# Node update in rounds of one chunk, gates gathered early, weighted rows of the first pass in PSUM

## What is computed

```python
msgs = z[edge_dst] @ Wd + z[edge_src] @ Ws + edge_weight[:, None] * ww[None, :] + bm
agg  = jax.ops.segment_max(msgs, edge_dst, num_segments=n)
hidden = relu(z @ W1a + where(deg > 0, agg, 0) @ W1b + b1)
x = layernorm(x + hidden @ W2 + b2)                  # node update, layer 0
h = x @ node_fc_W + node_fc_b                        # layer 1
a = sum(h[src] * h[dst]); alpha = seg_softmax(a, dst)
g = sigmoid(einsum(relu(he @ W1_m + b1_m), W2_m) + b2_m); beta = seg_softmax(g, dst)
h_att = segment_sum(alpha * (h[src] @ node_att_W[k]), dst) / 3
h_rel = segment_sum(sum_m beta_m * (h[src] @ rel_att_W[m]), dst) / 3
```

## Time and profile before

| | us |
|---|---|
| median of 3 runs | 2271.08 |
| lowest, highest | 2266.31, 2273.05 |
| profiled execution, its own time | 2279.13 |
| its span | 2277.4 |
| GpSimd busy | 1643.7 (72%) |
| TensorE busy | 1658.0 (73%) |
| VectorE busy | 1326.4 (58%) |
| ACT busy | 1119.3 (49%) |

### The profile page before, as it was taken

One profiled execution on the slowest core, in us unless ns is written; L12 is line 12 of the kernel. 1 busy time (PEld: TensorE's weight loads), 2 busy tenths in 40 slices (PEclk: granted clock), 3 DMA queues, 4 the chain that ended last, 5 costly groups with the idle time before them and its releaser, 6 DMA issues. The chain is left out here.

```text
span 2277.4 us, 43250 instructions
## 1 busy us (share of the span) xinstructions
PE 1658.0 (73%) x9891; PEld 1016.1 (45%) x9891; DVE 1326.4 (58%) x5220; ACT 1119.3 (49%) x3305; POOL 1643.7 (72%) x1705
## 2 busy tenths in 40 slices
PE   4687777778777887860767777776777776778774
PEld 4222222222232222210636666665666665667574
DVE  4665555555554444444656656666666666666559
ACT  1243433334434444540556656655565666556548
POOL 3777777777777777775657777777777777777625
PEclk7799999999988999985979988899888889888978
DMA  8634434343433343432432222222222222222214
GB/s 255 205 126 143 130 127 129 125 145 127 144 108 125 128 139 111 144 128 82 128 108 67 65 63 63 66 65 65 66 63 64 65 66 66 60 65 66 65 47 124
DMA packets 115983, 235.04 MB, mean 103 GB/s; under 512 B 32909, under 2 KB 68230, under 8 KB 106422
## 3 DMA queue, kind: packets, MB, share of 16 engines
q0 software_dynamic: 52832, 109.39, 19.9%
q1 hardware_dynamic: 56522, 97.21, 11.6%
q10 hardware_dynamic: 6540, 27.42, 3.4%
HBM read 166.01 MB, written 67.89 MB: 103 GB/s over the span
## 5 line engine op out<-in xcount | busy, mean ns | idle before, releaser
L209 POOL DMA_INDIRECT acc<-d_src_product,b_region x784 | 772.0, 985 | 239.4 <-issue 217.4
L463 POOL DMA_INDIRECT d_region<-d_h,d_region x784 | 758.1, 967 | 248.4 <-issue 216.1
L859 DVE SCALAR_TENSOR_TENSOR acc<-b_region,acc 128x128 f32<-128x128 f32 x784 | 271.7, 347 | 456.4 <-DMA acc<-d_src_product,b_region 456.1
L1577 DVE TENSOR_TENSOR acc<-acc,banks 128x160 f32 x784 | 252.6, 322 | 231.0 <-PE banks L1379 93.0
L651 PE MATMUL banks<-acc,b_region 64*128 64x512 f32 x1176 | 321.9, 655 | 38.3 <-ACT gate_col L756 17.9
L1345 PE MATMUL banks<-shift_ident,d_region 128*128 128x128 f32 x784 | 136.0, 299 | 240.7 <-DMA d_region<-d_h,d_region 231.6
L870 DVE SCALAR_TENSOR_TENSOR acc<-acc,b_region 128x128 f32<-128x128 f32 x784 | 270.2, 345 | 0.2 <-DVE acc L859 0.2
L1376 PE MATMUL banks<-d_region 128*128 128x128 f32 x1568 | 258.4, 319 | 0.0
L1379 PE MATMUL banks<-d_region,pick 128*128 128x128 f32 x1568 | 245.6, 307 | 0.0
L1376 PEld LDWEIGHTS banks<-d_region 128*128 128x128 f32 x1568 | 244.5, 236 | 0.7
L756 ACT ACTIVATE acc<-banks,b_region 128x1024 f32<-128x1024 f32 x147 | 158.8, 1112 | 167.9 <-PE banks L651 167.7
(11 more groups left out here) (261 smaller groups left out, 2394.4 us busy)
## 6 DMA issues: line engine op xcount, KB each, us to landing
d_runs<-acc SPq DMA_DIRECT2D x48, 1024.0 KB, 4.4
acc<-ea ACTq DMA_DIRECT2D x25, 1024.0 KB, 5.5
acc<-d_src_product,b_region POOLq DMA_INDIRECT x784
d_region<-d_h,d_region POOLq DMA_INDIRECT x784
d_region<-d_rel SPq DMA_DIRECT2D x49, 256.0 KB
hT<-xT SPq DMA_DIRECT2D x7, 448.0 KB, 6.9
d_src_product<-acc SPq DMA_DIRECT2D x7, 448.0 KB, 4.5
d_gates<-acc ACTq DMA_DIRECT2D x196, 6.0 KB
```

The costliest lines, as they stand in the source:

```text
L209: pool.indirect_dma_start(self.rows[:, s, j, :], None, d["B"], bass.IndirectOffsetOnAxis(self.idx[:, k:k + 1], 0)).then_inc(self.gathered[ ...
L463: pool.indirect_dma_start(rows[:, s, :], None, table, bass.IndirectOffsetOnAxis(idx[:, s:s + 1], 0)).then_inc(gathered[q], 16)
L859: nc.vector.scalar_tensor_tensor(rows[:, s, j, :], wwb, wgt[:, k:k + 1], rows[:, s, j, :], ALU.mult, ALU.add).then_inc(ch, 1)
L1577: nc.vector.tensor_tensor(w, w, UZ[q % 2][:, :, j, :], ALU.add).then_inc(ad, 1)
```

## The change

In the runs stage `step` writes its result into PSUM bank 0 (three buffers of 128 columns) and takes `ww` from the fourth quarter of that bank; `run` reads the row there. GpSimd waits for s_done of a step, no longer for r_done of a run, before it gathers into a group again. What TensorE kept in bank 0 beside the steps moves to banks 1 and 2.

In the node update every engine takes chunk n whole, then what follows the norm for chunk n - 1. GpSimd gathers the gates right after the run ends, without waits, into the same place as before; TensorE turns them at the head of the edge stage, and VectorE's second memset waits for that. In `gather_rows` the load of the iteration count comes after the first eight groups.

```diff
@@ gather_rows
-    rest = iterations_but_one(pool, t)
...
         if q == 0:
             after_first()
+    rest = iterations_but_one(pool, t)
     with pool.Fori(0, rest) as it:
@@ phase_runs
+        stepped = t["psum"][0][:, 0:STEPS * P].rearrange("p (s f) -> p s f", f=P)
+        wwp = t["psum"][0][:, STEPS * P:(STEPS + 1) * P]
...
+        def s_done(k):
+            return 2 * k if k else 1
...
-                    pool.wait_ge(ch, r_done(4 * (g - RG) + 3))
+                    pool.wait_ge(ch, s_done(GJ * (g - RG) + GJ - 1))
...
-                    last = nc.tensor.matmul(bank[0][:, k * P:(k + 1) * P], negH1[:, c * G4 + k * P:c * G4 + (k + 1) * P],
+                    last = nc.tensor.matmul(bank[1][:, k * P:(k + 1) * P], negH1[:, c * G4 + k * P:c * G4 + (k + 1) * P],
                                             w2n, start=True, stop=True)
...
                     pe.wait_ge(h2d, c)
-                    pe.wait_ge(gd, c)
+                    pe.wait_ge(h1c, c)
                 for k in range(z):
-                    nc.tensor.matmul(bank[0][:, k * P:(k + 1) * P],
+                    nc.tensor.matmul(bank[2][:, k * P:(k + 1) * P],
...
+            c.link(nc.vector.tensor_copy(wwp, wwb))
...
-                nc.vector.scalar_tensor_tensor(rows[:, s, j, :], wwb, wgt[:, k:k + 1], rows[:, s, j, :],
+                nc.vector.scalar_tensor_tensor(stepped[:, k % STEPS, :], wwp, wgt[:, k:k + 1], rows[:, s, j, :],
                                                ALU.mult, ALU.add).then_inc(ch, 1)
...
-                nc.vector.scalar_tensor_tensor(H[:, k % n, :], H[:, (k - 1) % n, :], rst[:, k:k + 1], rows[:, s, j, :],
-                                               ALU.add, ALU.max).then_inc(ch, 1)
+                nc.vector.scalar_tensor_tensor(H[:, k % n, :], H[:, (k - 1) % n, :], rst[:, k:k + 1],
+                                               stepped[:, k % STEPS, :], ALU.add, ALU.max).then_inc(ch, 1)
@@ phase_nodes0, sync
-            for c in range(NC4 + 3):
-                if c >= 3:
-                    store_h(c - 3)
-                if c < NC4:
-                    store_x1(c)
+            for c in range(NC4):
+                store_x1(c)
+                store_h(c)
@@ gpsimd
             for k in range(JC):
-                if k % 2 == 0:
-                    pool.wait_ge(hp, NC4 - JC // 2 + 1 + k // 2)
                 pool.indirect_dma_start(jg[:, k, :, :].rearrange("p m e -> p (m e)"), None, d["gates"][0:TC * P, :],
@@ tensor
-            for n in range(-3, NC4 + 2):
...
-            pe.wait_ge(jgs, 16 * JC)
...
-            turn_gates(*GATE_BANKS)
+            for n in range(NC4 + 1):
+                if n < NC4:
+                    turn_rows(n)
+                    hidden(n)
+                    out(n)
+                if n:
+                    turn_x1(n - 1)
+                    h_rows(n - 1)
@@ scalar
+            for n in range(NC4 + 1):
+                if n < NC4:
+                    copy_rows(n)
+                if n:
+                    norm(n - 1)
+                    copy_x1(n - 1)
+                if n < NC4:
+                    square_root(n)
@@ vector
+            for n in range(NC4 + 1):
+                if n < NC4:
+                    bound_hidden(n)
+                    stats_of(n)
+                if n:
+                    copy_h_rows(n - 1)
+                if n < NC4:
+                    shift(n)
@@ phase_edges, tensor
+            jg = gates_by_job(t)
+            pe.wait_ge(jgs, 16 * JC)
+            for s, b in enumerate(GATE_BANKS):
+                for k in range(4):
+                    last = nc.tensor.transpose(bank[b][:, k * P:(k + 1) * P], jg[:, s % 2 * 4 + k, s // 2, :], ident[:, :])
+                last.then_inc(gt, 1)
@@ scalar
             for s, b in enumerate(GATE_BANKS):
+                act.wait_ge(gt, s + 1)
@@ vector
             nc.vector.memset(acc[:, 0:2, :], 0.0).then_inc(zero, 1)
+            dve.wait_ge(gt, 2 * M)
             nc.vector.memset(acc[:, 2:5, :].rearrange("p a b -> p (a b)")[:, 0:(JC * M + NBLK) * P], 0.0
                              ).then_inc(zero, 1)
```

More of the change, by code:

```diff
@@ L497 @@
 HB = 3
+STEPS = 3
 LEASH = 4
@@ L686, in shifted_counts @@
                 pe.wait_ge(cnt, NBLK)
-                view = bank[0][:, 0:2 * NBLK].rearrange("p (a b) -> p a b", a=2)
+                view = bank[1][:, 0:2 * NBLK].rearrange("p (a b) -> p a b", a=2)
                 nc.tensor.matmul(view, t["shift"], cp, start=True, stop=True)
-                nc.tensor.matmul(bank[0][0:1, 2 * NBLK:4 * NBLK], ident[:, P - 1:P], cp, start=True, stop=True
+                nc.tensor.matmul(bank[1][0:1, 2 * NBLK:4 * NBLK], ident[:, P - 1:P], cp, start=True, stop=True
                                  ).then_inc(has, 1)
@@ L789, in _ @@
                         act.wait_ge(gd, c)
-                    nc.scalar.activation(hrep[:, 0:n], bank[0][:, 0:n], ACT.Copy).then_inc(hrc, 1)
+                    nc.scalar.activation(hrep[:, 0:n], bank[2][:, 0:n], ACT.Copy).then_inc(hrc, 1)
                 if 0 <= c < NC4 and off == 2:
@@ L893, in has_edges @@
                 c.link(nc.vector.scalar_tensor_tensor(total, cp[:, 0, :], float(EP), cp[:, 1, :], ALU.mult, ALU.add))
-                turned = bank[0][:, 0:4 * NBLK].rearrange("p (n a b) -> p n a b", n=2, a=2)
+                turned = bank[1][:, 0:4 * NBLK].rearrange("p (n a b) -> p n a b", n=2, a=2)
                 c.link(nc.vector.tensor_copy(cp, turned[:, 0, :, :]))
@@ L950, in blocks_view, with phase_nodes0 @@
     return bank[:, 0:(z - a) * P].rearrange("p (b f) -> p b f", f=P)
-def phase_nodes0(nc, new_sems, t, i, d):
+def phase_nodes0(nc, new_sems, t, i, d, jgs):
     with ExitStack() as ctx:
@@ L969, in phase_nodes0 @@
         fcbr = ca(P)
-        jg = cb(JC * M * P).rearrange("p (c m e) -> p c m e", c=JC, m=M)
+        cb(JC * M * P)
+        jg = gates_by_job(t)
         ends = cb(NBLK * P).rearrange("p (b f) -> p b f", f=P)
@@ L1074, in h_rows @@
                 last.then_inc(hp, 1)
[L1076 to L1080, removed]
-            for n in range(-3, NC4 + 2):
[L1083 to L1088, removed]
-                if 0 <= n - 1 < NC4:
-                    turn_x1(n - 1)
-                if 0 <= n - 2 < NC4:
-                    h_rows(n - 2)
-            pe.wait_ge(jgs, 16 * JC)
-            pe.wait_ge(mx, NC4)
-            pe.wait_ge(va, NC4)
-            pe.wait_ge(xtc, NC4)
-            turn_gates(*GATE_BANKS)
+            for n in range(NC4 + 1):
[4 more added lines that the diff above has]
+                if n:
+                    turn_x1(n - 1)
+                    h_rows(n - 1)
         @block.scalar
@@ L1130, in copy_x1 @@
                 nc.scalar.activation(x1T[:, c * G4:c * G4 + n], bank[4][:, 0:n], ACT.Copy).then_inc(xtc, 1)
-            for n in range(-3, NC4 + 2):
-                if n + 3 < NC4:
-                    copy_rows(n + 3)
-                if 0 <= n - 1 < NC4:
+            for n in range(NC4 + 1):
[3 more added lines that the diff above has]
+                    norm(n - 1)
                     copy_x1(n - 1)
-                if 0 <= n + 1 < NC4:
-                    square_root(n + 1)
-                    norm(n + 1)
+                if n < NC4:
+                    square_root(n)
         @block.vector
@@ L1197, in _ @@
             assert all(widths(c)[0] in (1, 2, 4) for c in range(NC4))
-            for n in range(-3, NC4 + 2):
-                if 0 <= n + 2 < NC4:
-                    bound_hidden(n + 2)
-                if 0 <= n + 1 < NC4:
-                    stats_of(n + 1)
-                if 0 <= n - 2 < NC4:
-                    copy_h_rows(n - 2)
-                if 0 <= n + 1 < NC4:
-                    shift(n + 1)
+            for n in range(NC4 + 1):
[6 more added lines that the diff above has]
+                    shift(n)
 def one_hot(nc, t, table, col, out):
@@ L1853, in build @@
             new_sems.phase_over()
-        phase_nodes0(nc, new_sems, t, i, d)
+        jgs, = new_sems.kept("gates_gathered")
+        phase_nodes0(nc, new_sems, t, i, d, jgs)
         new_sems.phase_over()
-        phase_edges(nc, new_sems, t, i, d)
+        phase_edges(nc, new_sems, t, i, d, jgs)
         new_sems.phase_over()
```

13 lines of the change are left out of this document (7 added, 6 removed).

## The result

The changed kernel takes **2251.53 us** (median of 22 executions, 2247.82 to 2291.8), the kernel before 2273.22 in the same company (22, 2262.77 to 2280.52): ratio 0.9905, interval 0.9896 to 0.9914, so 21.7 us faster. The profiled execution took 2248.64 for a span of 2246.9. Ratios leave out executions more than 1.5% above a kernel's fastest; of the change's 22 those are five, at 2285 to 2292, to which experiment 7 comes back.

What follows compares the result with a forecast made beforehand. GpSimd's queue of gathers was taken to bound the runs stage. Minus 29 (weighted rows), plus 10.5 (node update) and minus 0.5 (register load) made minus 19: 2260.1 us profiled, 2252 for the median, range 2238 to 2272.

Steps and rivals of the forecast that it cites:

- rival A: Whole kernel: the main forecast, unblocked gathers outweighing a slower node update, 2252 us, own range 2244 to 2262; 45%.
- Weighted rows in PSUM: Runs stage: with one SBUF tensor per step and run, gathers are no longer blocked; minus 29 us, ends 0 and minus 30.6.
- The price of PSUM operands: VectorE's steps and runs: reading or writing PSUM costs 0; other end 0.07 us more per operation.
- rival C: Runs stage: PSUM steps are longer and make gathers tied to the MLP late; plus 9, 2261 us; 15%.
- Earlier release, copy of the weights, bank moves: Runs stage: buffers freed after step, weights copied to PSUM, products in banks 1 and 2; worth nothing, hidden, and 0.
- Node update: One-chunk rounds bound by the chain of engines at 6.5 us, not gathers; plus 10.5 us, ends 0 and plus 44.
- the clock term: Node update: 2.1 rounds at TensorE's half clock, each 3.6 us longer; 7.5 us within the plus 10.5.
- Early gates: Seam between node update and edge stage: gates gathered beside the chain remove some 10 us, counted inside the node update's sum.
- Rival B: Node update: the chain keeps the gathers' pace; node update plus 2, 2244 us; 13%.
- D: Runs stage: gathers are still blocked, so only the seam counts; plus 10, 2281 us; 8%.
- F: Gathers: part of the excess stays through new alignments; 2258 to 2266 us; 10%.
- E: Node update: TensorE gets no full clock, all thirteen rounds at half clock; plus 44, 2286 us; 9%.

Runs made afterwards that it cites:

- experiment 7: The changed kernel with the edge stage's one-hots and iota also in PSUM: 2235.0 to 2281.3 us, ratio 0.9887 (first three) to the kernel before.
- experiment 1: The kernel before with only the change's runs stage (steps in PSUM, bank moves, earlier release): 2246.59 us, ratio 0.9881.
- run 337: Not a follow-up run: VectorE's `run` operation (running maximum) takes 337 ns in the changed kernel, against 345 in the kernel before.
- experiment 9: The changed kernel run once more, nothing edited: 2249.08 us, ratio 0.9888 to the kernel before.
- experiment 2: The changed kernel with the runs stage of the kernel before: 2276.3 to 2319.8 us, ratio 1.0040 (first four) to the kernel before.
- experiment 5: The changed kernel with step reading its weight from SBUF, still writing PSUM: 2260.78 us, ratio 0.9947 to the kernel before.
- experiment 6: The changed kernel with step in place in SBUF, weight from PSUM, run reading two SBUF tensors: 2258.6 to 2299.6 us, ratio 0.9954 (first three) to the kernel before.
- experiment 3: The kernel before with only the early gates and later load of the count, staggered node update kept: 2262.83 us, ratio 0.9959.
- experiment 4: The changed kernel with the node update's staggered loops and store order of the kernel before: 2236.35 us, ratio 0.9836 to the kernel before.
- experiment 10: The changed kernel with 32 and 30 idle TensorE products ahead of the node update: median 2283.76 us of twelve, ratio 0.9977 to the kernel before.
- experiment 8: The changed kernel with both the staggered node update and the edge stage's one-hots in PSUM: 2219.96 us, ratio 0.9770 to the kernel before.

## Why the prediction was right, and where its sizes were off

Forecast 2252, measured 2251.5, by the mechanism of rival A. That the numbers meet so closely is partly luck. The gain was forecast as 19 us and measured as 21.7; the kernel before stood at 2273.22 in the longer company and not at 2271.08, and the two differences nearly cancel. In the traces the sum was off by more: 2260.1 was forecast for the profiled execution, 2248.64 was measured. The two terms were off by 2 and by 5 us there, and another 5 came from the edge stage, which scatters.

**Weighted rows in PSUM: right.** Minus 29 was forecast, the trace has minus 30.7 for the stage, experiment 1 alone minus 27.3 in the medians. L209 fell to 945 where 946 to 950 was forecast, and of the ten gathers over 1.15 us one is left. The nearest row, L1577, was the right guide, though weaker than it was taken for: in the trace each of its four additions takes 322 ns and the next starts 0.45 us after it, so the gather beside them had gaps. The run of the change settles it: it reads one SBUF tensor and writes SBUF every 0.52 us with a step between, and doesn't block. The pointer scalar doesn't either; it stayed in SBUF. By the Trainium skill, "SBUF — State Buffer", section "Who interferes with whom", a VectorE instruction with two SBUF inputs contends with a GpSimd instruction that reads SBUF, and one with at most one, outside the modes that use both of VectorE's ports, doesn't. The fall from 985 to 945 agrees; no run shows which access of GpSimd is held up.

**The price of PSUM operands: right, 0.** Step 354 against 347, run 337 against 345: together 1 ns less. The other end, 0.07 us per operation (rival C), is excluded, and the leash never came into it: 6.3 us of waits against 5.3. That end was misread too: it set the time per addition of L1577 against the length of a step, and between one addition and the next lie 0.13 us in which the trace has register work, so it says nothing of an operand's price. By the Trainium skill, "VectorE: DVE Perf Modes", the TRN2 errata section, an operation from PSUM to SBUF has 120 cycles plus the elements where one from SBUF to SBUF has 58 plus the elements: 62 cycles more each time, as an estimate. The row of L875, 8 ns shorter than L870, disagrees with it for 128 columns of f32.

**Earlier release, copy of the weights, bank moves: 0, as forecast**, together. The runs part is the same 980.3 in experiment 1 and fits the blocked excess (784 x 40 ns = 31.4). They weren't tried one by one.

**Node update: the mechanism right, its cost too high for the traced execution.** Plus 10.5 less 0.5 was forecast, plus 4.9 measured (plus 6.6 in experiment 9, plus 9.9 in experiment 2). The round is 6.48, forecast 6.5; at half clock it is 3.6 longer, as forecast. What was too large is the clock term: "1.5 half-clock rounds at the start and 0.6 later: 2.1 x 3.6 = 7.5". Chunk 12 was turned 74.4 us after chunk 1 (1048.80 to 1123.19); eleven full-clock rounds are 71.3, so the clock cost 3.1 there. Past 1056.9 the stage stayed at full clock until the last chunk had been turned. This size is a lot too: the same eleven rounds cost 3.0 to 4.3 us over full clock in experiments 5, 6 and 9, 7.7 in experiment 2, which is the forecast, and 33 in experiment 7. The seam was 1.2 us shorter than the sum: the last row of h ends at 1132.0 and the first gather starts at 1135.46, 3.4 us instead of 4.6.

**Early gates: right.** "Some 10 us at the seam": experiment 3 has 10.1 in the node part and 11 in the medians, the register load among it; the 0.5 forecast for that load wasn't tried alone. The gates' gathers came 8 to 9 us later than forecast, as GpSimd now waits for the chain, and still 19 us before their use. The prediction had them only inside the sum and so did not say what the rounds cost alone. Experiment 4 does: 15 us. Its own row of 5.0 us per staggered round against 6.5 gives 12 x 1.5 = 18.

**Rival B** (chain keeps the pace) and **D** (still blocked) fell: 1.78 us waits of GpSimd in every chunk, and 945. **F** fell in the runs stage. **E**, at 9%, was put as all or nothing for the kernel. It fits single executions, as far as their totals tell: 5 of 22, at 2285 to 2292 against its 2286, and by the trace one in experiment 7 and one in experiment 10. What the argument missed is that "20 us at full clock right in this stage with gaps of 1 to 2 us" in one trace says nothing about the next execution.

**What would show it:** the rounds of 6.5 us, the end of the gathers near 1022 (1021.0) and the pitch of 0.26 came. Three gathers are over 1.1 us, the longest 1.21, where none was forecast, and L859 and L870 at 345 ns became 354 and 337. The edge stage's first gather starts 25.8 us earlier (1135.46 against 1161.26), forecast 19; the difference is the node term's 5 and the runs term's 2.

## What to carry to other kernels

Where a queue of indirect gathers sets the pace, look at VectorE's operations with two SBUF tensors before anything else on VectorE: moving one operand of each to PSUM cost VectorE nothing that shows here and gave 31 us of the traced runs stage (27 in the medians, experiment 1) and 16 in the other (experiments 4 and 8, 2236.35 to 2219.96). A stage that waits in turn on several engines is safer staggered: in experiment 1 three rounds wholly at half clock (1041.54 to 1056.40) took 4.95 us each, the pace of the gathers, though no staggered stage was seen at half clock to its end. Rounds of one chunk cost 15 us here and, in the two traced executions in which TensorE stayed at 1.2 GHz, 29 and 36 more. One trace shows one lot of the clock; the list of all executions shows how often it falls otherwise.

## What the runs showed of the hardware that was not expected

- The blocking isn't bound to one instruction. In the kernel before a gather begun in a chain of steps and runs took 3.39 us and ended 0.8 us after the chain's last; with every second operation off the path (experiments 5, 6) the mean excess over 945 is 8 and 15 ns, not half of 40, and no gather takes more than 1.24 us.
- A stage bound by a chain across engines ran 105 us at 1.2 GHz in one execution and for all but 30 us at 2.4 in another, with the same instructions in that stage (experiments 7 and 9). Full clock at the stage's start didn't hold it: experiment 10 had it for the stage's first 15 us, then 106 us at half, and nine of its twelve executions took 2277.9 or more.
- Writing PSUM from VectorE cost next to nothing: 355 ns from SBUF to PSUM against 347 from SBUF to SBUF, and the operation behind it took 340 against 345, so 3 ns for the pair.
